# A conditioned residual and a routed expert layer on one core: x turned by VectorE in squares of 32 instead of by TensorE

## What is computed

```python
def reference(x, cond_1024, base_layer, w1, b1, w2, b2, ln_g, ln_b, router_W, router_bias, s_w1, s_w3, s_w2, W1e, W2e):
    # first layer: a base matrix plus a rank-8 matrix for each of the 8 blocks
    ae = layernorm(cond_1024) * ln_g + ln_b
    xw = gelu(ae @ w1 + b1) @ w2 + b2
    x_a, x_b = (v.reshape(8, 512, 8) for v in split(xw, 2, axis=-1))
    layer = base_layer[None] + einsum('bdr,bkr->bdk', x_a, x_b)
    x = x + (x + einsum('btc,bco->bto', x, layer))
    # second layer: one shared network and 2 of 8 experts for each row
    shared = silu(x @ s_w1) * (x @ s_w3) @ s_w2
    s = sigmoid(concat([x, cond], -1) @ router_W)
    idx = top_k(s + router_bias, 2)
    gates = s[idx] / sum(s[idx])
    routed = sum over the two experts e of gates * (gelu(x @ W1e[e]) @ W2e[e])
    return x + (shared + routed) / 3
```

## Time and profile before

| | before |
|---|---|
| time, median of 3 runs | 1113.86 us (1112.78 to 1113.91) |
| the profiled execution: its span | 1114.8 us |
| TensorE busy | 1075.8 us, 97% of the span |
| VectorE busy | 483.5 us, 43% |
| ScalarE busy | 398.6 us, 36% |
| DMA, mean over the span | 172 GB/s |
| first layer, blocks 0 to 7 | up to 227.1 us of the span |

### The profile page before, as it was taken

How to read it: one execution, slowest core, us unless ns; L and a number is a source line. 1 busy time by engine, 2 the same in 40 slices (tenths; PEclk the granted TensorE clock), 3 DMA queues, 4 the chain that set the end, 5 groups by cost and what they waited for, 6 DMA issues and landing times.

```text
span 1114.8 us, 15416 instructions
## 1 busy us (share of the span) xinstructions
PE 1075.8 (97%) x5226; PEld 878.4 (79%) x5226; DVE 483.5 (43%) x1014; ACT 398.6 (36%) x687; POOL 154.2 (14%) x193
## 2 busy tenths in 40 slices
PE   7999899899699999999999999999999999999998
PEld 5666678688488888888888888888888888888886
DVE  3103654463356646655664533331424333142434
ACT  3212344351366566656656631211212121121211
POOL 2002267370000000000000022011020201102020
PEclk9999899999899999999999999999999999999999
DMA  8662589789768688767657445023050501305041
GB/s 308 263 255 72 187 296 395 277 295 306 204 191 263 210 246 267 223 191 218 203 152 201 174 135 205 1 60 129 0 188 0 188 0 59 130 0 188 0 151 38
DMA packets 131702, 191.42 MB, mean 172 GB/s; under 512 B 9534, under 2 KB 73022, under 8 KB 129878
## 3 DMA queue, kind: packets, MB, share of 16 engines
q1 hardware_dynamic: 120118, 156.38, 43.8%
q0 software_dynamic: 11552, 34.61, 8.3%
HBM read 117.04 MB, written 73.92 MB: 171 GB/s over the span
## 4 chain that ended last, share of the span: by engine, by line
PE 86%; DVE 5%; DMA 4%; SPq 3%; ACT 1%; issue 1%; DVEq 0%; ACTq 0%
PE K L1464 10%; PE K L1465 10%; PE K L1466 10%; PE L L1466 5%; PE L L1464 5%; PE L L1465 5%; PE Rb L1466 5%; PE Rb L1464 5%; PE Rb L1465 5%; PE M L1464 4%; PE M L1466 4%; PE M L1465 4%; PE Rb L1555 3%; PE M L1493 2%; PE M L1495 2%; PE M L1494 2%
## 5 line engine op out<-in xcount | busy, mean ns | idle before, releaser
L462 ACT ACTIVATE slf<-K 128x512 f32<-128x512 f32 x64 | 38.3, 598 | 219.7 <-PE K L1466 219.0
L775 POOL DMA_INDIRECT yb<-ys_d,pos_fix x64 | 61.3, 958 | 321.4 <-DVE total L1395 253.3
L465 ACT CAST gTh<-slf 128x512 fp32r<-128x512 f32 x64 | 39.8, 621 | 183.0 <-DVE slf L475 183.0
L1464 PE MATMUL M<-w2h,gTh 128*128 128x512 f32 x256 | 99.7, 389 | 0.5 <-DVE gTl L477 0.5
L1464 PE MATMUL K<-x1h,w13h 128*128 128x512 f32 x256 | 99.7, 389 | 0.0
L1466 PE MATMUL K<-x1h,w13l 128*128 128x512 f32 x256 | 99.6, 389 | 0.0
L1465 PE MATMUL M<-w2l,gTh 128*128 128x512 f32 x256 | 99.6, 389 | 0.0
L1466 PE MATMUL M<-w2h,gTl 128*128 128x512 f32 x256 | 99.6, 389 | 0.0
L1465 PE MATMUL K<-x1l,w13h 128*128 128x512 f32 x256 | 99.6, 389 | 0.0
L475 DVE TENSOR_TENSOR slf<-L,slf 128x512 f32<-128x512 f32 x32 | 22.1, 691 | 155.9 <-PE L L1466 150.8
L1332 DVE TENSOR_TENSOR e2l<-e2raw,e2h 128x512 fp32r<-128x512 f32 x64 | 41.3, 687 | 79.3 <-ACT e2h L929 79.3
(11 more groups left out here) (248 smaller groups left out, 2469.4 us busy)
## 6 DMA issues: line engine op xcount, KB each, us to landing
w2c<-in_L_cond_w_dram SPq DMA_DIRECT2D x8, 2048.0 KB, 8.4
e1raw<-in_L_cond_W1e_dram SPq DMA_DIRECT2D x16, 1024.0 KB, 7.2
e2raw<-in_L_cond_W2e_dram SPq DMA_DIRECT2D x16, 1024.0 KB, 5.6
xr<-xs_d SPq DMA_DIRECT2D x64, 256.0 KB, 4.6
ys_d<-yo SPq DMA_DIRECT2D x32, 512.0 KB, 7.3
xtok<-in_x_dram SPq DMA_DIRECT2D x32, 256.0 KB, 7.4
x_d<-x1tok SPq DMA_DIRECT2D x8, 1024.0 KB, 8.1
xs_d<-zeros SPq DMA_DIRECT2D x8, 1024.0 KB, 8.4
```

The source lines that it names most:

```text
L462: nc.scalar.activation(slf[:, h % 2], U[h % 2][:], ACT.Silu).then_inc(ffn.silu, 1)
L465: nc.scalar.copy(gTh[:, h % 2], slf[:, h % 2]).then_inc(ffn.g_hi, 1)
L775: pool.indirect_dma_start(out=yb[:, c, :], out_offset=None, in_=ys_d, in_offset=bass.IndirectOffsetOnAxis(ap=pos_fix[:, c:c + 1].bitcast(U ...
L1464: mm(o, ah, bh_, start=start, stop=False)
```

## The change

x is no longer turned by TensorE. SP loads a whole block as quarters of rows with four DMAs (32 partitions by 16 pieces of 128 numbers each), as `load_rows` does it for the experts; block 1 has a buffer of its own. VectorE turns each tile by squares of 32 (`turn_x`) into one of two SBUF buffers, from which ScalarE and VectorE make the high and the low part. With this, chunk c of the channels holds the channels 128 j + 32 c + f on partition 32 j + f. So the rows of the base matrix are loaded in that order, its diagonal is at another place (now added by GpSimd, with a matrix `twice`), and the rank-8 factors are needed once in the old order (`XW`) and once in the new (`XWq`).

```diff
-        X_AFTER = {2: 0, 4: 1, 5: 2, 6: 3}
+        TURN_AT, HI_AT, LO_AT = {1: 0, 2: 1, 3: 2, 4: 3}, {2: 0, 3: 1, 4: 2, 5: 3}, {2: 0, 3: 1, 4: 2, 5: 3}
+        def x_rows(b):
+            return x[b].rearrange("(n t) (j f) -> j t n f", t=32, j=4)
...
-        K_USES = [("x", 0, 0), ("x", 0, 1)] + [("x", b, t) for b in range(1, EARLY) for t in range(TT)]
-        K_USES += [("x", 3, 0), ("x", 3, 1), ("t", 0, 0), ("t", 0, 1), ("x", 3, 2), ("x", 3, 3), ("t", 0, 2), ("t", 0, 3)]
+        K_USES = [("t", 0, 0), ("t", 0, 1), ("t", 0, 2), ("t", 0, 3)]
...
-            def load_x(b, t):
-                sp.wait_ge(xt_ps, (b - 1) * TT + t + 1)
-                sp.dma_start(xtok[:, t], x_view[:, b * TT + t, :]).then_inc(x_in[t], 16)
+            def load_x(b):
+                if b > 1:
+                    sp.wait_ge(xq_f, (1 if b == 2 else b) * TT)
+                for j in range(4):
+                    sp.dma_start(quarters(b)[32 * j:32 * j + 32].rearrange("p t i f -> p (t i) f"), x_rows(b)[j]
+                                 ).then_inc(x_in[b % 2], 16)
...
-                    if half in (2, 4, 5, 6) and b + 2 < NB:
-                        load_x(b + 2, (2, 4, 5, 6).index(half))
+                    if half == 4 and b + 2 < NB:
+                        load_x(b + 2)
...
+            for k in range(KC):
+                v = basep[:, k].rearrange("p (j c f) -> p c j f", j=4, c=KC)[:, k]
+                nc.gpsimd.tensor_tensor(v, v, twice[:].rearrange("p (j f) -> p j f", j=4), ALU.add).then_inc(diag, 1)
...
+            def turn_x(b, t):
+
+                dve.wait_ge(x_in[b % 2], 64 * (b // 2 + 1))
+                if (b, t) in ((EARLY, 0), (EARLY, 1)):
+                    dve.wait_ge(cond_ps, LOADS)
+                elif b > 0 or t > 1:
+                    dve.wait_ge(xt_lo, b * TT + t - 1)
+                nc.vector.transpose(turned(b)[:, t % 2].rearrange("p c (i n) -> p i c n", i=4),
+                                    quarters(b)[:, t].rearrange("p i (c f) -> p i c f", c=KC)).then_inc(xq_f, 1)
...
-            for k in range(KC):
-                v = basep[:, k, k * P:(k + 1) * P]
-                nc.vector.scalar_tensor_tensor(out=v, in0=ident[:], scalar=2.0, in1=v,
-                                               op0=ALU.mult, op1=ALU.add).then_inc(diag, 1)
...
+            tt(XWq[:].rearrange("p k (j f) -> p k j f", j=4), by_quarters(XWP), by_quarters(biasXW), ALU.add).then_inc(xw_f, 1)
...
-                bank = k_bank("x", b, t)
-                for c in range(KC):
-                    last_mm = nc.tensor.transpose(bank[:, c * P:(c + 1) * P], xtok[:, t, c * P:(c + 1) * P], ident[:])
-                last_mm.then_inc(xt_ps, 1)
...
-                    if h in X_AFTER and b + 1 < NB:
-                        xtr(b + 1, X_AFTER[h])
```

More of the change, by code:

```diff
@@ L113, in build @@
             b2v = sb("b2v", [P, 2, KC, RK], F32, st)
+            with ExitStack() as z:
+                XWq = sb("XWq", [P, KC, P], F32, z)
             b2rep = sb("b2rep", [P, KC, P], F32, st)
@@ L157, in build @@
         with ExitStack() as st:
+            with ExitStack() as z:
+                twice = sb("twice", [P, P], F32, z)
             upper = sb("upper", [P, P], F32, st)
@@ L278, in build @@
         wsl = sem("wsl")
-        x_in = [sem(f"x_in{t}") for t in range(TT)]
-        xt_ps = sem("xt_ps")
+        x_in = [sem(f"x_in{i}") for i in range(2)]
+        xq_f = sem("xq_f")
         xt_hi = sem("xt_hi")
@@ L358, in build, with by_quarters, quarters, turned @@
         D_VAR, D_AE, D_AET, D_HPRE, D_HT, D_TBS, D_TB = 3, 8, 9, 10, 14, 16, 17
-        X_AFTER = {2: 0, 4: 1, 5: 2, 6: 3}
+        TURN_AT, HI_AT, LO_AT = {1: 0, 2: 1, 3: 2, 4: 3}, {2: 0, 3: 1, 4: 2, 5: 3}, {2: 0, 3: 1, 4: 2, 5: 3}
+        def x_rows(b):
+            return x[b].rearrange("(n t) (j f) -> j t n f", t=32, j=4)
+        def by_quarters(v):
+            return v[:].rearrange("p (j k f) -> p k j f", j=4, k=KC)
+        def quarters(b):
+            return xtok if b != 1 else x1tok0[:].rearrange("p t (i f) -> p t i f", i=4)
+        def turned(b):
+            return xt_early if b < EARLY else xt_late
         def t_after(b):
@@ L858, in _ @@
             keep_turned(3)
+            act.wait_ge(d0, D_TB)
+            xt_hi_(2, 0)
+            xt_hi_(2, 1)
             keep_base(1, 2)
+            xt_hi_(2, 2)
+            xt_hi_(2, 3)
             keep_base(1, 3)
-            act.wait_ge(d0, D_TB)
-            for t in range(TT):
-                xt_hi_(2, t)
             act.wait_ge(base_lo, KC)
@@ L1167, in _ @@
             assert n0[0] == D_TB
-            xt_lo_(1, 2)
-            xt_lo_(1, 3)
-            for t in range(TT):
-                xt_lo_(2, t)
+            turn_x(2, 0)
+            turn_x(2, 1)
+            turn_rest(2)
             dve.wait_ge(cond_ps, LOADS)
@@ L1571, in _ @@
             last_mm.then_inc(p0, 1)
-            for t in range(TT):
-                xtr(0, t)
             base_half(0, 0, 0)
@@ L1603, in _ @@
             cond_net(1)
-            xtr(1, 2)
-            xtr(1, 3)
             pe.wait_ge(d0, D_TB)
@@ L1646, in _ @@
             last_mm.then_inc(xwt_ps, 1)
+            pe.wait_ge(xw_f, 2)
+            for k in range(KC):
+                last_mm = nc.tensor.transpose(K[0][:, k * P:(k + 1) * P], XWq[:, k], ident[:])
+            last_mm.then_inc(xwt_ps, 1)
             base_half(2, 2, 1)
@@ L1661, in _ @@
             scores(0)
-            xtr(3, 0)
-            xtr(3, 1)
             corr(0, 0)
@@ L1675, in _ @@
             corr(1, 3)
-            xtr(3, 2)
-            xtr(3, 3)
             tok(0, 2)
```

123 lines of the change are left out of this document (67 added, 56 removed).

## The result

The changed kernel takes 1121.51 us (median of 5 runs, 1119.49 to 1122.59) beside 1113.91 us for the kernel before (5 runs): a ratio of 1.0063, 95% interval 1.0044 to 1.0081. I had forecast 1113.2 us, within a range of 1108.8 to 1118.0. So "no change" was wrong, and the time lies outside the range.

A forecast was written before the change was run, and what follows sets the result against it. The first layer was taken as a chain between TensorE, ScalarE, VectorE and the DMA queue; terms summed to -0.7 us, less 0.9 between span and median: 1113.2 us against 1113.86, range 1108.8 to 1118.0.

The forecast's parts named there:

- no change: Whole kernel: the time stays within 2.2 us (about 0.2%) of before; chance 0.42.
- Start: To the first base product: x lands at about 8.3 us, then VectorE works without a gap until 17.1; +4.1 us.
- The 2.4 us more for a block of x: Loads of x: as quarters of rows at 208 GB/s, a block takes 5.0 us and not 2.6.
- Network and XWq: Condition's network, 13 to 102.7 us: eight transpose groups leave TensorE, -6.9; four more transposes for XWq, +0.4.
- Corrections: From 102.7 to 122.8 us: two turns delay VectorE's low parts, on which TensorE waits; +1.2 us, bounds 0 and +2.5.
- Block 3: Four tiles are turned behind `weigh`, ending at 145.6 us, so `scores(4)` comes later than 144.3; +1.2 us.
- Block 5: TensorE has less work, but block 6's x lands at about 172.9 us and sets `scores(6)` at 182.4; +0.7 us.
- Block 4: TensorE's work plus 2.4 us for ScalarE's stand gives 20.1 us instead of 23.3; -3.2 us, bounds 18 and 22.5.
- Block 6: Block 7's x, issued at 181.0 us, lands at 195.6; tiles and pieces put `scores(7)` at 206.5; +1.8 us.
- rival B: Block 6: block 7's x lands still later, 20 us after issue, `scores(7)` at 211.2; 1117.9 us, slower; chance 0.24.
- Whatever the first layer gains or loses arrives at the end undiminished: Stages behind 227.1 us: untouched, they just shift with the first layer's end; 0 us.
- Rival A: Blocks 5 and 6: the loads cost nothing, x lands as before; -4.6 us, 1109.3 us, faster; chance 0.34.

The follow-up runs named there:

- mixed kernels: Changed kernel with another feature order, TensorE turning all blocks (1.0068 of before) or all but 1 and 2 (1.0009; 0.9962 with the base layer into 128 partitions).
- the second trace: The changed kernel itself, unaltered, traced again on another chip of the first kind: 1120.3 us, 1.0048 of the kernel before.
- the fourth batch: Ratios to before, first-kind chip: changed kernel 1.0048; its x in 2 KB rows 1.0023; quarter turns in blocks 4 to 7 1.0035; only blocks 1 and 2 by VectorE 0.9995.

## Why the prediction was wrong

**Start (+4.1, measured +4.9 and +4.8 in two traces): right in kind; x landed 0.8 later than I had it.** In ten traces with block 0 turned by VectorE (all but the one of strided turns and the one of the base layer chunk by chunk) the first base product stands 8.8 to 9.1 us behind x's landing (forecast 8.8), so VectorE's list was as described and sets the start. What I left out was the base layer. I read the diff's new transfers as the same bytes in the same 2 KB pieces and gave them no row; into 32 partitions each they land some 3 us later, and alone would put the first base product at 17.6 us. That it cost nothing here, and that the diagonal on GpSimd (0.57 us a chunk, within the bounds) cost nothing, is luck: the first chunk was ready at 14.3 us, and ScalarE and VectorE came to it at 15.4 and 16.5. The mechanism that I used for x had a gap of the same sort: I put the 208 GB/s of the earlier trace rows down to the short pieces, and those transfers also go into 32 partitions, which is most of it. The 2.4 us more for a block of x hold for the transfers as they are, with the wrong reason.

**Network and XWq (-6.5, measured -6.9): right.** The two mixed kernels that differ in blocks 1 and 2 alone are 6.5 us apart in their medians.

**Corrections (+1.2, +2.0):** right in kind. The low parts wait behind turns. The clock adds to it, which I had not counted: from `scores(1)` to `scores(2)` the granted clock was 0.54 (0.90 before), and TensorE was busy for 7.1 us with work that took 4.8. With the turns doubled this stage grew again, by 2.2 us.

**Block 3 (+1.2, +0.9): right. Block 5 (+0.7, +1.0): right in size,** with two errors that cancel: x was there 9.9 us behind the block's start and not 8.5, and `scores(6)` came 8.5 us behind that and not 9.5.

**Block 4 (-3.2, +0.4): this step failed.** It reads "ScalarE now stands at the first high part until the turn behind `weigh`...; I leave 2.4 us for that: 20.1". I took TensorE's work and the wait that I could see, and did not ask when piece 2 would land. In block 5 and 6 I did ask that of x. Now x(5) goes out only when block 4's last turn is done, at 143.9 us, in one batch of slow transfers with two stores of 1 MB behind it; piece 2 is issued at 156.8 and takes 8.8 us to land; in the trace of before it was issued at 155.2, took 3.9, and nobody waited for it. In the second trace, where the block takes 21.67 us, 1.5 less than before, TensorE waits 2.68 us at that place instead of 4.31:

```profile
166.52 0.63 PE L1587 MATMUL K<-ident,xp 128*128 128x128 f32 x4 [2.68 <-ACT x1tok L849]
```

20.1 came in neither. The table of block 4 above shows that the missing term is this wait: less the wait for piece 2 the block is 18.8 us in three traces and 18.0 and 19.1 in the other two, inside the forecast's bounds; with x in rows of 2 KB and a wait of 1.3 us it is 20.1; and three quarters of the turns' work taken away leave it at 21.8. The block's miss is 3.6 us in the first trace and 1.7 in the second, the largest single term of the 6.6 by which that first trace misses the forecast (+5.9, not -0.7). The rest is the start and the corrections, 0.8 each, and 2.1 behind block 7, less what block 7 gained.

**Block 6 (+1.8, +2.1):** the size was right, rival B's landing (behind 199.2 us) is what came: x(7) was there at 202.8. But its clause was 18.2 us from the issue, and it took 16.9; the rest is that the issue was 5 us later than forecast, at 186.0. The misses of the start, the corrections and block 4 stand behind that.

**"Whatever the first layer gains or loses arrives at the end undiminished":** not refuted (+0.8 to the first group, +1.3 behind it, in one trace; 0.7 in the other), but inside the first layer a lead shrinks on its way: the three kernels of the fourth batch that reached `scores(6)` 3.2 to 4.6 us before the changed kernel reached the feed-forward 0.7 to 1.5 us before it. Why the stages behind 227 us took 0.7 and 2.1 us more, no run shows.

**Rival A** fell with the rates: the loads did cost, 3.0 us in all beside rows of 2 KB into 128 partitions, though which of the 3.0 us the 32 partitions cost and which the 512 B, no run shows; of the rate the 32 partitions take most. **Rival B** has the sign. It gave 4.0 us over before, with block 4 at its forecast -3.2; with block 4 at +0.4 the same sum is 7.6, what was measured. With the second trace's -1.5 it is 5.7, so that agreement is partly luck.

**The clock.** The mean granted clock of all runs of the fourth batch is 0.9828 for the changed kernel and 0.9859 for before. Within the executions of one kernel a lower clock goes with a longer span, by 0.5 to 0.8 us for 0.001 in the six of ten kernels on chips of the first kind where the correlation is -0.7 to -0.9. In the two compared here it is looser: 0.3 us with a correlation of -0.3 for the changed kernel, 0.5 with -0.5 for before. So the difference of 0.0031 could stand for 0.9 to 1.9 us of the 5.2. That is a correlation; no run set the clock.

**Open:** why the chips of the second kind are slower in blocks 4 and 7, and why the change pays there. On them ScalarE stands where the bank was filled long before. Of the kernel before, in block 4:

```profile
161.73 1.05 ACT L792 CAST w13h<-wraw 128x1024 fp32r<-128x1024 f32 x1
167.20 0.58 ACT L808 COPY xp<-M 128x512 f32<-128x512 f32 x1 [4.42 <-remote]
```

The copy needs a bank that TensorE had done by 163.2 us. The profile names what released the copy only as `remote`. Such stands of ScalarE sum to 11.5 to 28.2 us from 118 to 250 us in the eight traces of the second kind, and to 0 in those of the first. Open too: why the clock was lower in blocks 3 and 4 of the kernel that led when x wasn't transferred, and whether the longer block 6 of all mixed kernels (24.6 to 26.0 us, 22.3 before) is the order's or the spread's, since there is one trace of the kernel before from the first kind.

## What to carry to other kernels

When a change alters how data comes in, price every transfer of the diff by how many partitions it fills and by its piece size, also those whose bytes and pieces look the same, and before you read a rate from a window check which transfer is in it. When a load now waits for the last step of a block instead of the first, ask of each transfer behind it in the queue, block by block, when it lands and who stands in line behind its reader. Work moved from a full engine to one whose list has gaps is paid at the places where that list is already waited for; here blocks 1 and 2, turned early, gave 6.5 us beside a control with the same order of features, and the later blocks together gave nothing on chips of the first kind.
